# Another order for the end of a fused cross-attention kernel: turned maxima, normalised tiles, moments and gammas

## The chip, the cores and the metric

The kernel runs on one core of a Trainium2 chip. The metric is the device time of one execution in microseconds (us); the kernel's time is the median of several executions. A core has five engines that work side by side, each through its own instructions in order, and meet through semaphores: PE (TensorE, matrix products), DVE (VectorE), ACT (ScalarE), POOL (GpSimd) and SP (SyncE, here only for transfers). ACT issues a few transfers of its own.

## The reference

Cross-attention of 4 batches with 1024 queries, 64 keys and 16 heads of 16, then the output projection, the residual and a layer normalisation, all in float32:

```python
Q = _split_heads(jnp.einsum('bsd,ed->bse', query, w_q) + b_q)
K = _split_heads(jnp.einsum('bsd,ed->bse', key, w_k) + b_k)
V = _split_heads(jnp.einsum('bsd,ed->bse', value, w_v) + b_v)
scores = jnp.einsum('bhqd,bhkd->bhqk', Q, K) / jnp.sqrt(jnp.float32(D_K))
scores = jnp.where(mask[:, None, :, :] == 0, jnp.float32(-1000000000.0), scores)
attn = jax.nn.softmax(scores, axis=-1)
ctx = jnp.einsum('bhqk,bhkd->bhqd', attn, V)
ctx = ctx.transpose(0, 2, 1, 3).reshape(B, SQ, D_MODEL)
out = jnp.einsum('bsd,ed->bse', ctx, w_o) + b_o + residual
mu = jnp.mean(out, axis=-1, keepdims=True)
var = jnp.mean(jnp.square(out - mu), axis=-1, keepdims=True)
out = (out - mu) * jax.lax.rsqrt(var + LN_EPS) * ln_gamma + ln_beta
```

## The kernel before

The 4096 queries are cut into 8 chunks of 512 (CHUNKS; LAST is 7), each of 4 tiles of 128 queries. A chunk's 16 heads come in two groups, j = 0 and 1; "(c, j)" below is group j of chunk c. A chunk passes through these steps, several chunks being under way at once:

- PE projects the queries (project_queries, L361). ACT copies them out of PSUM (queries_out, queries_beside).
- max_scores(c, i), L406, gives the scores of one tile and group as queries by keys in a PSUM bank, eight per chunk (i = 0 to 7). DVE takes the maximum over the keys (maxima(c, i), L771). When all eight are there, PE turns the maxima (turn_max, L418, four transposes), and ACT copies them out negated (negative_max, L674, tile neg).
- PE makes the scores again as keys by queries: scores_on_mask (L445, L451), then scores_less_max (L458) adds the negated maxima. Where under(g) holds, the mask isn't added by PE (L445): ACT copies it into the four banks (mask_under, L668) as they come free behind the exponentials of the group before. ACT takes the exponentials in four quarters (exponentials(c, j), L658).
- PE multiplies with the values (values, L474). DVE turns the result (turn_out, L791), takes reciprocals, divides (L805) and turns the parts for the output product (L811): divide(c, j).
- PE applies wo (output(c, i, t), L500; i is a pair of tiles and t one of the pair). DVE adds the residual (residual(c, i), L819) and takes mean and variance (moments(c, i): two bn_stats L831, two bn_aggr L835).
- POOL makes rstd and shift out of these (deviations, L1003 to L1009), ACT applies them tile by tile (normalised(c, order), L681), POOL multiplies by gamma (L1023) and adds beta (L1026) for a pair of tiles (affine(c, i)), and SP stores.
- POOL also adds the output bias to x (with_bias, L994).

The steady loop runs over s from 0 to 5 on PE, DVE and POOL. Its pass s works on chunk s's scores, on the maxima of chunk s + 1, and on the outputs and normalisation of the chunks before. After it, the last steps are written out by hand, line by line, for each engine. The order on an engine is that of the code; an instruction waits for its semaphores and holds up everything behind it.

The last chunk is done otherwise at its end: the identity product of last_input (L513) brings x into PSUM, last_output adds the output product there, DVE takes the moments from PSUM, and centred (L841) and scaled (L851) do the normalisation on DVE. last_deviations on POOL gives the rstd. Of chunk 6, POOL does gammas and betas for tiles 0 and 1, and DVE (gammas, L858; betas, L864) for tiles 2 and 3, out of a PSUM copy of both rows that ACT makes once divide(7, 1) is over (L735). The stores of chunk 6 are issued by ACT (L739, L741), those of chunk 7 by SP (L266).

Waits that matter for the order: turn_max waits for all maxima of its chunk; output(5, 0) waits for all maxima of chunk 7; output(5, 1) for the neg of chunk 7; max_scores(7, 2) for maxima(7, 1); normalised(c, order) for the deviations of its tiles; last_input(0) and values(7, 1) for all exponentials; DVE's gammas for all normalised tiles of chunk 6.

Of the kernel before, what the change touches and what calls it, by code (L numbers as in the profile page):

```python
# [43 lines left out]
def build(nc, xT, x, maskT, ctxT, wq, wk, wv, wo, bias_rows, consts, out):  # L44
    with ExitStack() as ctx:
# [96 lines left out]
        stored = [sem(f"stored{i}") for i in range(2)]  # L142

        LAST = CHUNKS - 1
# [161 lines left out]
        def _(pe):  # L306
# [105 lines left out]
            def turn_max(c):  # L412
                pe.wait_ge(nm_done, HALVES * (c + 1))
                if c == 0:
                    pe.wait_ge(in_con, 16)
                    pe.wait_ge(kt_done, 2)
                for t in range(TILES):
                    mm = pe.transpose(ps_w[:, 1, t * P:(t + 1) * P], nmax[:, c % 2, t], con[:, IDENT:IDENT + P])  # L418
                mm.then_inc(turn_done, 1)
# [5 lines left out]
            def scores_on_mask(c, j):  # L425


                g = 2 * c + j
                b = c // PER_BATCH
                if g == 0:  # L430
                    pe.wait_ge(qe_done, 3)
                    pe.wait_ge(nm_done, HALVES)
                    pe.wait_ge(const_done, 2)
                    pe.wait_ge(kpair_done, 1)
                else:
                    if g == 1:
                        pe.wait_ge(kpair_done, 2)
                    pe.wait_ge(qe_done, g + 1)
                if not under(g):
                    if g:  # L440
                        pe.wait_ge(e_done, QUADS * g)
                    pe.wait_ge(mask_done, masks_done(c))
                    for quad in range(QUADS):
                        r = rows(quad % 2)
                        pe.matmul(ps_s[:, quad], key_rows[r].rearrange("p h k -> p (h k)"), mask[r, c % NM],  # L445
                                  start=True, stop=False)
                for quad in range(QUADS):
                    r = quad_rows(quad)
                    if under(g):
                        pe.wait_ge(under_done, QUADS * unders(g) + quad + 1)  # L450
                    pe.matmul(ps_s[:, quad], k_pair[r, b, j].rearrange("p h k -> p (h k)"), q_sb[r, c % NQ, j],  # L451
                              start=False, stop=False, skip_group_check=under(g))

            def scores_less_max(c, j):
                pe.wait_ge(neg_done, c + 1)
                for quad in range(QUADS):
                    r = slice(32 * quad, 32 * quad + 4)
                    pe.matmul(ps_s[:, quad], select[r, j].rearrange("p h k -> p (h k)"), neg[r, c % 2],  # L458
                              start=False, stop=True, skip_group_check=under(2 * c + j)).then_inc(s_done, 1)
# [126 lines left out]
            max_scores(LAST, 5)  # L586
            max_scores(LAST, 6)
            max_scores(LAST, 7)
            scores_on_mask(LAST, 0)
            output(LAST - 2, 0, 0)  # L590
            turn_max(LAST)
            output(LAST - 2, 0, 1)
            scores_less_max(LAST, 0)
            values(LAST - 1, 1)
            output(LAST - 2, 1, 0)
            output(LAST - 2, 1, 1)
# [12 lines left out]
        def _(act):  # L609
# [11 lines left out]
            def queries_out(c, j):  # L621
                act.wait_ge(q_done, 2 * c + j + 1)
                if c >= NQ:
                    act.wait_ge(s_done, PAIRS * (c - NQ + 1))
                    act.wait_ge(max_done, HALVES * (c - NQ + 1))
                act.activation(q_sb[:, c % NQ, j], query_bank(c, j), ACT.Identity,  # L626
                               bias=con[:, BIAS + j:BIAS + j + 1]).then_inc(qe_done, 1)
# [24 lines left out]
            def exponentials(c, j):  # L652
                g = 2 * c + j
                if g >= 2:
                    act.wait_ge(pv_done, PAIRS * (g - 1))
                for quad in range(QUADS):
                    act.wait_ge(s_done, QUADS * g + quad + 1)
                    act.activation(probs[:, g % 2, quad], ps_s[:, quad], ACT.Exp).then_inc(e_done, 1)  # L658
                    if quad and under(g + 1):
                        mask_under(g + 1, quad - 1)  # L660
                if under(g + 1):
                    mask_under(g + 1, QUADS - 1)
# [13 lines left out]
            def normalised(c, order=range(TILES)):  # L676
                act.wait_ge(ln_done, deviations_done(c, 2 in order))
                if c >= 2:
                    act.wait_ge(stored[c % 2], 16 * (c // 2))
                for t in order:  # L680
                    act.activation(y[:, c % 2, t], res[:, c % 2, t], ACT.Identity, bias=shift[:, c % 2, t:t + 1],  # L681
                                   scale=rstd[:, c % 2, t:t + 1]).then_inc(y_done, 1)
# [25 lines left out]
            for s in range(CHUNKS):  # L708
                exponentials(s, 0)
                if s < LAST:  # L710
                    queries_beside(s + 1, 1)
                if s == 0:
                    queries_out(2, 0)
                if s < 2:
                    high_x(s + 3)
                if 1 <= s and s + 2 < CHUNKS:
                    queries_out(s + 2, 0)
                exponentials(s, 1)
                if s + 2 < CHUNKS:
                    queries_beside(s + 2, 0)  # L720
                if s >= 2 and s + 3 < CHUNKS:
                    high_x(s + 3)
                if s == LAST:
                    normalised(LAST - 2, (0, 1))
                    normalised(LAST - 2, (2, 3))
                elif s == LAST - 1:
                    normalised(s - 2)
                if s + 2 < CHUNKS:
                    queries_out(s + 2, 1)
                if s + 1 < CHUNKS:  # L730
                    negative_max(s + 1)
                if 2 <= s < LAST - 1:
                    normalised(s - 2)
            act.wait_ge(div_done, GROUPS)
            act.activation(ps_s[:, 1].rearrange("p (n d) -> p n d", d=D), brow[:, 2:4], ACT.Copy).then_inc(gb_done, 1)  # L735
            normalised(LAST - 1, (0, 1))
            normalised(LAST - 1, (2, 3))
            act.wait_ge(dve_bet_done, 1)
            act.dma_start(out[LAST - 1, :, 2:4], y_of(LAST - 1)[:, 2:4]).then_inc(stored[(LAST - 1) % 2], 16)  # L739
            act.wait_ge(bet_done, 2 * LAST - 1)  # L740
            act.dma_start(out[LAST - 1, :, 0:2], y_of(LAST - 1)[:, 0:2]).then_inc(stored[(LAST - 1) % 2], 16)  # L741

        @block.vector
        def _(dve):
# [149 lines left out]
            for s in range(LAST - 1):  # L894
                front = s + 1
                maxima(front, 0)
                if s >= 2:
                    moments(s - 2, 0)
                maxima(front, 1)
                maxima(front, 2)  # L900
                if s >= 2:
                    residual(s - 2, 1)
                    turn_out(s - 1, 1)
                elif s == 0:
                    value_blocks()
                maxima(front, 3)
                if s >= 2:
                    divide_turned(s - 1, 1)
                elif s == 1:
                    divide(0, 1)  # L910
                maxima(front, 4)
                if s >= 2:
                    moments(s - 2, 1)
                maxima(front, 5)
                if s >= 1:
                    residual(s - 1, 0)
                maxima(front, 6)
                maxima(front, 7)
                divide(s, 0)
            maxima(LAST, 0)  # L920
            moments(LAST - 3, 0)
            maxima(LAST, 1)
            divide(LAST - 2, 1)
            residual(LAST - 3, 1)
# [27 lines left out]
        def _(pool):  # L952
# [65 lines left out]
                pool.tensor_tensor(rstd[:, i], veps[:, i], half_neg[:], ALU.pow).then_inc(ln_done, 1)  # L1018

            def affine(c, i):  # L1020
                two = slice(2 * i, 2 * i + 2)
                pool.wait_ge(y_done, TILES * c + 2 * i + 2)
                pool.tensor_tensor(y[:, c % 2, two], y[:, c % 2, two], brow[:, 2].unsqueeze(1).to_broadcast([P, 2, D]),  # L1023
                                   ALU.mult).then_inc(gam_done, 1)
                pool.wait_ge(gam_done, 2 * c + i + 1)
                pool.tensor_tensor(y[:, c % 2, two], y[:, c % 2, two], brow[:, 3].unsqueeze(1).to_broadcast([P, 2, D]),  # L1026
                                   ALU.add).then_inc(bet_done, 1)
# [43 lines left out]
            affine(LAST - 3, 0)  # L1071
            affine(LAST - 3, 1)
            deviations(LAST - 2, slice(0, 2))
            deviations(LAST - 2, slice(2, 4))
            affine(LAST - 2, 0)
            affine(LAST - 2, 1)
            deviations(LAST - 1, slice(0, 2))
            deviations(LAST - 1, slice(2, 4))
            last_deviations()
            affine(LAST - 1, 0)  # L1080


# [47 lines left out]
```

## Time and profile before

| | |
|---|---|
| time, median of 3 executions | 154.56 us (154.33 to 154.88) |
| the profiled execution | 154.85 us, of which the span of the profile is 153.3 us |
| busy, share of the span | PE 87%, DVE 81%, ACT 76%, POOL 68% |
| chain that ended last | PE 44%, DVE 27%, issue 8%, ACT 8%, DMA 5%, POOL 4% |
| granted PE clock | full until 146 us, half after it |

The span runs from the first instruction to the last event; about 1.5 us of the execution lie around it. Times of rows are from the start of the span. A busy share is an average over stages with different limits: the kernel's last fifth has to be read by itself. "Issue" in the chain is time in which the engine waited for nothing that the profile shows. The ends of matrix products are modelled, and spans on POOL are rough.

### The profile page before, as it was taken

The numbers are of one execution on the slowest core, as the hardware profiler recorded it, in microseconds if no ns is written. First come the engines' busy times: TensorE is split into PE (matmuls) and PEld (weight loads), VectorE is DVE, ScalarE is ACT, GpSimd is POOL, SyncE is SP. The second block draws the span as 40 slices with busy tenths as digits, with TensorE's granted clock in tenths as the row PEclk, the third lists the DMA queues.
The fourth block names the chain that finished last, engine by engine and source line by source line (L and its number), as shares of the span: only waits on it lengthen the run. The fifth ranks groups of instructions, "written<-read, shape, count | busy, mean of one in ns | idle before, by whom it ended". The sixth has DMA issues, their size and how long they took to land.

```text
span 153.3 us, 2741 instructions
## 1 busy us (share of the span) xinstructions
PE 133.6 (87%) x900; PEld 80.4 (52%) x900; DVE 123.8 (81%) x232; ACT 116.5 (76%) x210; POOL 103.9 (68%) x107
## 2 busy tenths in 40 slices
PE   0799997978899999999999999999988999999500
PEld 0586745453565656555665565546535355368400
DVE  0098938577878899898989898989899997999991
ACT  3269988898688878999999989999796786271320
POOL 6003738583499502399949999999849999479590
PEclk9999999999999999999999999999999999999955
DMA  4997299999953230029700570027300620300306
GB/s 139 322 283 208 50 275 236 266 290 266 218 209 73 80 122 19 0 85 266 265 6 0 139 261 14 2 56 220 137 0 4 175 98 0 141 0 0 137 17 259
DMA packets 8382, 20.46 MB, mean 133 GB/s; under 512 B 1073, under 2 KB 1329, under 8 KB 8369
## 3 DMA queue, kind: packets, MB, share of 16 engines
q1 hardware_dynamic: 7648, 19.14, 43.3%
q10 hardware_dynamic: 720, 1.15, 2.2%
q8 instruction: 7, 0.11, 0.3%
q14 instruction: 7, 0.05, 0.1%
HBM read 12.43 MB, written 4.19 MB: 108 GB/s over the span
## 4 chain that ended last, share of the span: by engine, by line
PE 44%; DVE 27%; issue 8%; ACT 8%; DMA 5%; POOL 4%; SPq 2%; DVEq 1%; POOLq 0%; ACTq 0%
PE ps_w L500 10%; PE ps_w L406 9%; DVE nmax L771 8%; PE ps_s L451 6%; PE ps_s L474 5%; DMA wv_sb<-wv 5%; DVE turned L791 5%; PE ps_w L361 5%; DVE stat L831 4%; DVE div_t L805 3%; PE ps_s L458 3%; DVE res L819 2%; ACT probs L658 2%; DVE cn L811 2%; PE ps_s L445 2%
## 5 line engine op out<-in xcount | busy, mean ns | idle before, releaser
L771 DVE TENSOR_REDUCE nmax<-ps_w 128x8 f32<-128x512 f32 x56 | 37.5, 677 | 14.0 <-PE ps_w L406 13.4
L658 ACT ACTIVATE probs<-ps_s 128x512 f32<-128x512 f32 x64 | 35.4, 597 | 11.6 <-PE ps_s L458 11.6
L958 POOL TENSOR_TENSOR xt_l<-xt_sb,xt_h 128x1024 fp32r<-128x1024 f32 x7 | 16.6, 2370 | 24.0 <-DVE k_half L759 10.9
L406 PEld LDWEIGHTS ps_w<-k_half,q_mask 128*128 128x128 f32 x112 | 16.8, 188 | 26.8 <-DVE nmax L771 20.8
L406 PE MATMUL ps_w<-k_half,q_mask 128*128 128x256 f32 x112 | 27.1, 331 | 4.1 <-DVE nmax L771 3.5
L500 PE MATMUL ps_w<-wo_sb,cn 128*128 128x256 f32 x112 | 29.0, 387 | 0.5
L668 ACT ACTIVATE ps_s<-mask 128x512 f32<-128x512 f32 x44 | 25.8, 612 | 0.0
L500 PEld LDWEIGHTS ps_w<-wo_sb,cn 128*128 128x128 f32 x112 | 19.4, 189 | 6.4 <-issue 2.7
L791 DVE STREAM_TRANSPOSE turned<-ps_s 128x1024 f32<-128x1024 f32 x16 | 19.9, 1242 | 0.1
L994 POOL TENSOR_TENSOR x_sb<-x_sb,brow 128x1024 f32<-128x1024 f32 x8 | 19.0, 2378 | 1.0 <-DMA x_sb<-x 0.8
L451 PE MATMUL ps_s<-q_sb,k_pair 32*128 32x512 f32 x128 | 19.3, 640 | 0.0
L1023 POOL TENSOR_TENSOR y<-y,brow 128x512 f32<-128x512 f32 x13 | 16.6, 1278 | 3.2 <-ACT y L681 3.0
L643 ACT ACTIVATE q_mask<-q_sb 64x512 fp32r<-64x512 f32 x28 | 17.6, 629 | 0.4
L474 PE MATMUL ps_s<-probs,v_bd 64*32 64x512 f32 x256 | 17.4, 601 | 0.0
L1026 POOL TENSOR_TENSOR y<-y,brow 128x512 f32<-128x512 f32 x13 | 16.6, 1276 | 1.0
L681 ACT ACTIVATE y<-res,shift,rstd 128x256 f32<-128x256 f32 x28 | 14.6, 596 | 2.3 <-POOL shift L1009 2.3
L811 DVE STREAM_TRANSPOSE cn<-div_t 128x512 f32<-128x512 f32 x16 | 11.4, 711 | 0.6
L626 ACT ACTIVATE q_sb<-ps_w,con 128x512 f32<-128x512 f32 x13 | 8.9, 682 | 3.3 <-PE ps_w L361 3.2
L805 DVE TENSOR_TENSOR div_t<-turned,ps_s 128x512 f32<-128x512 f32 x16 | 10.9, 683 | 0.4
L361 PE MATMUL ps_w<-xt_h,wq_h 128*128 128x512 f32 x26 | 10.6, 408 | 0.3 <-DVE nmax L771 0.3
L458 PE MATMUL ps_s<-neg,select 4*128 4x512 f32 x64 | 10.5, 643 | 0.4 <-ACT neg L674 0.3
L819 DVE TENSOR_TENSOR res<-ps_w,x_sb 128x512 f32<-128x512 f32 x14 | 9.5, 677 | 1.4 <-PE ps_w L500 0.9
(79 smaller groups left out, 198.2 us busy)
## 6 DMA issues: line engine op xcount, KB each, us to landing
x_sb<-x SPq DMA_DIRECT2D x8, 512.0 KB, 4.8
xt_sb<-xT SPq DMA_DIRECT2D x7, 512.0 KB, 5.1
q_mask<-mask SPq DMA_DIRECT2D x12, 256.0 KB, 4.1
out<-y SPq DMA_DIRECT2D x6, 512.0 KB, 2.6
m_sb<-maskT SPq DMA_DIRECT2D x16, 128.0 KB, 6.2
xt_sb<-xT SPq DMA_DIRECT2D x2, 256.0 KB, 5.6
q_mask<-mask SPq DMA_DIRECT2D x4, 128.0 KB, 2.3
out<-y ACTq DMA_DIRECT2D x2, 256.0 KB, 2.3
```

Of the source, the lines that this page charges most:

```text
L361: mm = pe.matmul(query_bank(c, j), w[:, d, j * P:(j + 1) * P], a[:, c % 2, d], start=d == 0 and w is wq_h and a is xt_h, stop=d == PC - 1 ...
L406: mm = pe.matmul(max_bank(c, i)[:, half * 256:half * 256 + 256], q_mask[:, c % 2, half, j, t * P:(t + 1) * P], k_half[:, b % 2, half, j].r ...
L451: pe.matmul(ps_s[:, quad], k_pair[r, b, j].rearrange("p h k -> p (h k)"), q_sb[r, c % NQ, j], start=False, stop=False, skip_group_check=un ...
L474: pe.matmul(values_banks(g)[quad_rows(quad), h], v_bd[rows(h), b, QUADS * j + quad], probs[rows(h), g % 2, quad], start=True, stop=True).t ...
L500: return pe.matmul(tile_outputs(c, i)[:, t], cn[:, c % 2, j, (2 * i + t) * P:(2 * i + t + 1) * P], wo_sb[:, j], start=j == 0 and c < LAST, ...
L643: act.activation(q_mask[r, c % 2, half, j], q_sb[r, c % NQ, j], ACT.Copy).then_inc(qdir_done, 1)
L658: act.activation(probs[:, g % 2, quad], ps_s[:, quad], ACT.Exp).then_inc(e_done, 1)
L668: act.activation(ps_s[:, quad], mask[:, g // 2 % NM].bitcast(F32), ACT.Copy).then_inc(under_done, 1)
L771: dve.tensor_reduce(nmax[:, c % 2, t].rearrange("p (q r) -> p q r", r=32)[:, :, 2 * j:2 * j + 2], max_bank(c, i).rearrange("p (q h k) -> p ...
L791: dve.transpose(turned[:, 0:2 * CHUNK], values_banks(g).rearrange("p h n -> p (h n)")).then_inc(pturn_done, 1)
L958: pool.tensor_tensor(xt_l[:, c % 2], xt_sb[:, c % 2], xt_h[:, c % 2].bitcast(F32), ALU.subtract).then_inc(xl_done, 1)
L994: pool.tensor_tensor(x_sb[:, c % 3], x_sb[:, c % 3], brow[:, 1].unsqueeze(1).to_broadcast([P, TILES, D]), ALU.add).then_inc(xb_done, 1)
```

## The change

In the steady loop DVE takes moments(4, 0) in pass s = 5, between maxima(6, 6) and maxima(6, 7), and not after maxima(7, 0). On PE, turn_max(7) follows max_scores(7, 7) at once, and both parts of scores(7, 0) come after output(5, 0). On ACT, normalised(4) comes behind the neg copy of chunk 7 and not ahead of it; the first two tiles of chunk 5 are normalised ahead of exponentials(7, 1), the other two behind it as before; the stores of the two halves of chunk 6 change places. On POOL, affine is split into gammas and betas, and in chunks 5 and 6 the gammas of the first pair run between the two sets of deviations, the betas behind the second set (in chunk 6 behind last_deviations).

```diff
 PE:
             max_scores(LAST, 7)
-            scores_on_mask(LAST, 0)
+            turn_max(LAST)
             output(LAST - 2, 0, 0)
-            turn_max(LAST)
             output(LAST - 2, 0, 1)
-            scores_less_max(LAST, 0)
+            scores(LAST, 0)
             values(LAST - 1, 1)
 ACT:
+                if s == LAST:
+                    normalised(LAST - 2, (0, 1))
                 exponentials(s, 1)
...
                 if s == LAST:
-                    normalised(LAST - 2, (0, 1))
                     normalised(LAST - 2, (2, 3))
-                elif s == LAST - 1:
-                    normalised(s - 2)
...
                     negative_max(s + 1)
-                if 2 <= s < LAST - 1:
+                if 2 <= s < LAST:
                     normalised(s - 2)
...
+            act.wait_ge(bet_done, 2 * LAST - 1)
+            act.dma_start(out[LAST - 1, :, 0:2], y_of(LAST - 1)[:, 0:2]).then_inc(stored[(LAST - 1) % 2], 16)
             act.wait_ge(dve_bet_done, 1)
             act.dma_start(out[LAST - 1, :, 2:4], y_of(LAST - 1)[:, 2:4]).then_inc(stored[(LAST - 1) % 2], 16)
-            act.wait_ge(bet_done, 2 * LAST - 1)
-            act.dma_start(out[LAST - 1, :, 0:2], y_of(LAST - 1)[:, 0:2]).then_inc(stored[(LAST - 1) % 2], 16)
 DVE:
                 maxima(front, 6)
+                if s == LAST - 2:
+                    moments(s - 1, 0)
                 maxima(front, 7)
                 divide(s, 0)
             maxima(LAST, 0)
-            moments(LAST - 3, 0)
             maxima(LAST, 1)
 POOL:
             def affine(c, i):
+                gammas(c, i)
+                betas(c, i)
...
             deviations(LAST - 2, slice(0, 2))
+            gammas(LAST - 2, 0)
             deviations(LAST - 2, slice(2, 4))
-            affine(LAST - 2, 0)
+            betas(LAST - 2, 0)
             affine(LAST - 2, 1)
             deviations(LAST - 1, slice(0, 2))
+            gammas(LAST - 1, 0)
             deviations(LAST - 1, slice(2, 4))
             last_deviations()
-            affine(LAST - 1, 0)
+            betas(LAST - 1, 0)
```

## Rows read from the trace of the kernel before

**Rows 1.** The page: the chain of work that ended last, shares by engine.
```profile
PE 44%; DVE 27%; issue 8%; ACT 8%; DMA 5%; POOL 4%; SPq 2%; DVEq 1%; POOLq 0%; ACTq 0%
```
**Rows 2.** Busy time by stretch: us, engines' busy time, clock, DMA share, GB/s.
```profile
128.15:141.30 13.15, 13.15 (x101) 8.00 (x92) 12.52 (x26) 6.07 (x12) 10.01 (x14) 1.00 0.11 41
```
**Rows 3.** Timeline, DVE: start, duration, line, operation, tiles, [idle before].
```profile
109.72 0.69 DVE L771 TENSOR_REDUCE nmax<-ps_w 128x8 f32<-128x512 f32 x1 [0.65 <-PE ps_w L406]
...
113.93 0.73 DVE L831 BATCH_NORM_STATS2 stat<-res 128x6 f32<-128x256 f32 x2
...
114.86 0.66 DVE L771 TENSOR_REDUCE nmax<-ps_w 128x8 f32<-128x512 f32 x1
...
120.57 3.34 DVE L771 TENSOR_REDUCE nmax<-ps_w 128x8 f32<-128x512 f32 x5
```
**Rows 4.** Timeline, PE, around the turn of chunk 6's maxima.
```profile
110.89 0.60 PE L418 MATMUL ps_w<-con,nmax 128*128 128x128 f32 x4
...
115.58 0.51 PE L406 MATMUL ps_w<-k_half,q_mask 128*128 128x256 f32 x2 [1.07 <-DVE nmax L771]
```
**Rows 5.** Timeline, PE and DVE, after the last maxima.
```profile
126.17 0.60 PE L418 MATMUL ps_w<-con,nmax 128*128 128x128 f32 x4
...
127.67 0.69 DVE L819 TENSOR_TENSOR res<-ps_w,x_sb 128x512 f32<-128x512 f32 x1 [0.74 <-PE ps_w L500]
...
128.00 1.09 PE L474 MATMUL ps_s<-probs,v_bd 64*32 64x512 f32 x16
...
129.02 1.99 PE L500 MATMUL ps_w<-wo_sb,cn 128*128 128x256 f32 x8
```
**Rows 6.** Timeline, PE, ACT and DVE, last scores to last divide.
```profile
131.61 1.14 PE L451 MATMUL ps_s<-q_sb,k_pair 32*128 32x512 f32 x8
...
132.91 1.09 PE L474 MATMUL ps_s<-probs,v_bd 64*32 64x512 f32 x16
133.06 2.07 ACT L658 ACTIVATE probs<-ps_s 128x512 f32<-128x512 f32 x4 [2.85 <-PE ps_s L458]
...
134.29 1.25 DVE L791 STREAM_TRANSPOSE turned<-ps_s 128x1024 f32<-128x1024 f32 x1
...
135.76 1.03 PE L513 MATMUL ps_s<-x_sb,con 128*128 128x256 f32 x4
...
138.96 1.22 DVE L791 STREAM_TRANSPOSE turned<-ps_s 128x1024 f32<-128x1024 f32 x1
```
**Rows 7.** Timeline, POOL: chunk 4's gammas and betas, chunk 5's first deviations.
```profile
125.48 1.28 POOL L1023 TENSOR_TENSOR y<-y,brow 128x512 f32<-128x512 f32 x1
...
128.06 1.29 POOL L1023 TENSOR_TENSOR y<-y,brow 128x512 f32<-128x512 f32 x1
...
129.43 1.27 POOL L1026 TENSOR_TENSOR y<-y,brow 128x512 f32<-128x512 f32 x1
...
130.78 0.19 POOL L1003 TENSOR_SCALAR veps<-mv 128x2 f32<-128x2 f32 x1
...
132.11 0.19 POOL L1009 TENSOR_TENSOR shift<-nmean,rstd 128x2 f32<-128x2 f32 x1
```
**Rows 8.** Timeline, POOL, ACT and DVE: the last deviations, tiles and gammas.
```profile
141.46 0.19 POOL L1003 TENSOR_SCALAR veps<-mv 128x2 f32<-128x2 f32 x1
...
143.78 0.19 POOL L1003 TENSOR_SCALAR veps<-mv 128x2 f32<-128x2 f32 x1 [0.79 <-DVE mv L835]
...
145.32 1.09 ACT L681 ACTIVATE y<-res,shift,rstd 128x256 f32<-128x256 f32 x2 [1.21 <-POOL shift L1009]
...
145.91 1.01 POOL L1018 TENSOR_TENSOR rstd<-veps,half_neg 128x4 f32<-128x4 f32 x1
...
147.01 0.68 DVE L858 TENSOR_TENSOR y<-y,ps_s 128x512 f32<-128x512 f32 x1
```
**Rows 9.** Timeline, ACT's first store; then busy time by stretch, the stores' end.
```profile
148.44 0.36 ACTq L739 DMA_DIRECT2D out<-y  x1
...
152.00:152.30 0.30, 0.00 (x0) 0.00 (x0) 0.00 (x0) 0.00 (x0) 0.00 (x0) 0.50 0.47 171
```

More of the change, by code:

```diff
@@ L1020, in affine, with gammas @@
             def affine(c, i):
+                gammas(c, i)
+                betas(c, i)
+            def gammas(c, i):
                 two = slice(2 * i, 2 * i + 2)
@@ L1024, in affine, with betas @@
                                    ALU.mult).then_inc(gam_done, 1)
+            def betas(c, i):
+                two = slice(2 * i, 2 * i + 2)
                 pool.wait_ge(gam_done, 2 * c + i + 1)
```

## The prediction

> **What bounds the kernel now.** I read the page first, for the order of size: three engines are busy for three quarters of the span or more, and the chain of work that ended last is mostly PE and DVE, with POOL at 4% [rows 1]. An average of that kind can't price a change to the last fifth of the kernel, so I went on to the busy time by stretch, then to the timeline of each engine from 94 us on, and last to the waits. In the stretch from 128.15 to 141.30 DVE works 12.52 of 13.15 us and PE all 13.15, ACT and POOL much less [rows 2]. What to see in the timeline is which engine has no gap: after the wait of 0.74 us at 127.67 [rows 5] DVE runs nearly without one to the last scaled tiles, and the end is DVE's: chunk 6's gammas at 147.01, then betas, then the two scaled pairs, then the stores [rows 8, 9]. POOL stands idle in several places in that end. It therefore costs nothing today, and what I have to find out is whether it still costs nothing in the new order.
>
> **Chunk 4's moments a step sooner.** The pair of moments takes a slot of 0.93 us (113.93 to 114.86) [rows 3]. In its new place, before maxima(6, 7), DVE sat idle for 0.65 us waiting for PE [rows 3]. So 0.65 of it is hidden and maxima(6, 7) moves back by 0.28, to end at 110.69. The turn_max behind it starts at 110.89 because PE is busy with projections until then [rows 4], so 0.2 us of cover is left and it isn't late. If that cover were gone, the delay would be that of neg and the scores of chunk 6, behind which PE has a wait anyway. Later, maxima(7, 1) comes 0.93 - 0.28 = 0.65 earlier. PE waited 1.07 us for just that at 115.58 [rows 4], so the whole row behind it (output of chunk 4, scores of chunk 6, exponentials, maxima(7, 2) to (7, 7)) moves with it: the last maximum ends at 120.57 + 3.34 - 0.65 = 123.26 instead of 123.91 [rows 3]. Bounds: 0, if the later steps are held elsewhere, and 0.93. I take 0.65, because the idle time is on the row itself. SP's load of the last x waits for a residual of this row and comes earlier too; nobody is late for it.
>
> **Last maxima turned at once.** turn_max goes ahead of the scores on mask and of output(5, 0, 0). It starts at 123.30 instead of 126.17 and takes 0.60 [rows 5]. The neg copy starts on ACT at 123.94. ACT now has normalised(4) behind it and not ahead. ACT instructions follow each other at 0.49 us (four exponentials in 2.07 [rows 6]), so chunk 4 is normalised from 124.43, its first two tiles at 1.09 [rows 8] are there at 125.52, and POOL, with a hand-over of 0.08, begins affine(4, 0) at 125.60. Before it was 125.48 [rows 7]. **This is the first cost: 0.12 us on POOL**, although everything ahead came 0.65 earlier, since normalised(4) lost its place ahead of neg.
> On PE, output(5, 0) runs from 123.9 for 1.99 us at most (a pair of tiles in [rows 5]) to 125.8, and the 0.74 us that DVE stood still for residual(5, 0) vanish. Then the scores of (7, 0): exponentials follow the start of scores by 1.45 and values by 1.30 (131.61 to 133.06 and 132.91 [rows 6]), so values(6, 1) begins at 127.0 to 127.2 instead of 128.00 [rows 5]: 0.8 to 1.0 earlier. DVE took values(7, 0) 1.38 after they began (134.29 against 132.91 [rows 6]); with the whole PE row 0.8 to 1.0 earlier, it now takes them at 133.3 to 133.5, and would be ready for divide(7, 1) at 138.0 to 138.2 instead of 138.96 [rows 6].
>
> **Chunk 5's tiles ahead of the last scores' exponentials.** ACT is idle 2.85 us before exponentials(7, 1) [rows 6], and the two activations go there. But they wait for the deviations of (5, 0), which POOL begins only behind affine(4): 125.60 + (130.78 - 125.48 = 5.30) = 130.90, and the shift ends 1.52 later (130.78 to 132.11 plus 0.19 [rows 7]) at 132.42. The two tiles then run from 132.46 and exponentials(7, 1), which could have begun at 132.1 to 132.3, are queued behind them until 133.44: 0.38 later than the 133.06 of before. They end at 135.51. The identity products of last_input(0) (1.03 [rows 6]) and 1.38 for the values give DVE its data at about 137.9, when DVE itself is ready at 138.0 to 138.2. So the queueing is just covered; that cover is 0.1 to 0.3 us. DVE's own end is then about 0.8 early. But last_input(0) starts at 135.55 instead of 135.76 [rows 6], so PE's row to the last output products is 0.2 early only, and DVE's last moments have to wait for them; between 0.2 and 0.8 I estimate 0.5, which lets DVE's gammas start at 146.5.
>
> **GpSimd's gammas between deviations.** From 132.42 I follow POOL. Prices: gamma to its beta 1.37 (128.06 to 129.43), beta to the next gamma 1.21 (2.58 from gamma to gamma, 125.48 to 128.06, less 1.37), to the next deviations 1.35 (129.43 to 130.78), a set of deviations 1.52 [rows 7]. Tiles (5, 0) normalised at 133.55, gammas(5, 0) from 133.63; deviations(5, second) 134.98 to 136.50; betas(5, 0) 136.5; gammas(5, 1) 137.72, betas(5, 1) 139.09; deviations(6, first) 140.44 to 141.96. Before, POOL lost time here in waits for DVE and ACT, and this set began at 141.46 [rows 8]: 1.0 is gained. ACT normalises from 142.00 to 143.09. And now the new order takes it back: gammas(6, 0) stand ahead of the second deviations, wait for ACT and run from 143.17; **deviations(6, second) begins at 144.52 where it began at 143.78** as soon as DVE's means were there [rows 8]. They end at 146.04, ACT normalises the last two tiles at 146.08 to 147.17 (before from 145.32), and DVE's gammas, which wait for these, start at 147.22 instead of 147.01 [rows 8]. Behind that wait DVE's betas and all of the last chunk's scaling are queued: **+0.21 us**. The limit at the end has changed from DVE to the round POOL, ACT, POOL, ACT, DVE.
> For a gamma followed by deviations there is no row; I took beta to deviations, 1.35. The nearest ends are 1.21 and 1.37, for two places -0.28 to +0.04. The Trainium skill (GPSIMD Engine Reference, on completion under the instruction's steps) says that completion holds back what waits on the instruction's semaphore and not the next Pool instruction; by that the veps behind a gamma, which doesn't depend on it, would start at the short distance and the sum would be -0.07 instead of +0.21. The row of beta to deviations, where nothing depends either, shows 1.35, so I keep the row's number.
>
> **The stores.** ACT now issues the store of tiles 0 and 1 of chunk 6 first, and it waits for betas(6, 0), which POOL runs last: 146.04, then 0.27 to rstd, 1.01 for it [rows 8] and 1.27 for the betas = 148.6, and the other half queues behind that. The first store before went at 148.44 [rows 9]. The four stores then run back to back until 152.3 [rows 9], so a first issue 0.2 later moves the end by as much, the same as DVE's part; the two are side by side, not added.
> By the Trainium skill (DMA: Bandwidth & Descriptors, on the fixed cost) each transfer has about 2.0 us fixed and 436 GB/s, so 0.25 MB issued last ends 2.6 us after its issue however early the others went. By that, an early DVE alone would bring the end forward even if POOL's store is late.
>
> **Sum.** On the profiled execution of 154.85 us: + 0.21 = 155.06. That execution stands 0.29 us above the median of 154.56, so 154.77, rounded 154.8 us, 0.1% more.
>
> **Rivals.** (1) *Faster: POOL doesn't hold the end.* DVE goes on at 146.5, gain 0.5: 154.05. It needs the round above to be 0.72 us shorter than my sum; the short distances of POOL give 0.28 and the best case of the moved moments 0.28 (0.93 instead of 0.65), together 0.56, so only with both and something more. At 0.56 alone the time is 154.2. Against it are POOL's durations, which hardly vary. (2) *Slower: the step of moments gives nothing.* Place: the wait of 1.07 at 115.58. If PE or ACT holds the row behind it, the last maximum stays at 123.91, neg, normalised(4) and POOL's whole series shift one for one, and the end is 0.21 + 0.65 = 0.86 later: 155.4. It decides (over 155.02) from a saving below 0.40 instead of 0.65. The cover of 0.2 at 110.89 and PE's gap of 1.07 speak against it. (3) *It cancels:* 154.55, with POOL's distances short, gains and losses nearly zero. (4) *The exponentials become the bound:* exponentials(7, 1) later than about 134.5 instead of 133.44 would make DVE the last again; POOL would then be late itself, so it is a part of (2).
>
> **Numbers.** My forecast (154.65 to 155.02) 0.40; (3) and down to 154.10, 0.17; (1) below 154.10, 0.17; (2) above 155.02, 0.26. A measurement here can tell 0.3%, 0.46 us, from nothing: faster is below 154.10, slower above 155.02. The range for 8 in 10 is 154.05 to 155.45, from rival (1) to rival (2).
>
> **What would show it.** Right: turn_max directly after the last maximum, near 123.3; no gap on DVE before residual(5, 0); exponentials(7, 1) near 133.4 behind two activations of L681's kind that waited for POOL's shift; POOL without a gap from 125.6 to 132.4; deviations(6, second) near 144.5; a DVE gap of about 0.8 near 146.5, ended by ACT's y; first store at 148.6. Wrong: no such gap and gammas before 146.8 (then rival 1), or maxima(7, 7) still ending at 123.9 (rival 2).

## The result, and the profile after

The changed kernel took 155.19 us in the median of 22 executions (154.19 to 156.25), the kernel before beside it 154.52 (154.24 to 156.11): ratio 1.0043, 95% interval 1.0022 to 1.0063. By that number the change costs 0.66 us. The forecast was 154.8, +0.21, within 154.05 to 155.45. So the range holds, the sign is right, and the size is three times the forecast. The trace shows that these 0.66 us have two sources.

The page of the changed kernel's profiled execution (156.25 us, span 154.7), the slices of granted PE clock and the chain that ended last by engine:

```profile
PEclk9999997899999999999999999999999999999965
...
PE 38%; DVE 24%; POOL 11%; issue 9%; ACT 8%; DMA 5%; SPq 2%; DVEq 1%; POOLq 0%; ACTq 0%
```

Two things are new. POOL's share of the chain is 11% where it was 4% [rows 1]: that is the change. And there is a 7 in the clock line near a sixth of the span, far ahead of all changed code. Busy time by stretch shows it, first this trace, where the clock is 1.00 at full rate (2.4 GHz) and 0.5 at half (1.2 GHz):

```profile
21.00:25.00 4.00, 3.05 (x21) 1.51 (x20) 1.69 (x3) 3.41 (x8) 3.51 (x3) 1.00 0.97 283
25.00:29.00 4.00, 4.00 (x16) 2.79 (x20) 2.26 (x4) 2.45 (x4) 1.22 (x3) 0.57 1.06 260
```

The granted clock is at half from 25.1 to 28.5 us here; PE was busy 3.05 of the 4.00 us before. The projection products take 0.63 us each in that stretch instead of 0.40. What it costs is read from the first of them to the scores behind them, this trace first, then that of before:

```profile
24.85 0.58 PE L361 MATMUL ps_w<-xt_h,wq_h 128*128 128x512 f32 x1 [0.29 <-DVE nmax L769]
...
30.13 0.73 PE L406 MATMUL ps_w<-k_half,q_mask 128*128 128x256 f32 x4
```
```profile
25.06 0.47 PE L361 MATMUL ps_w<-xt_h,wq_h 128*128 128x512 f32 x1 [0.29 <-DVE nmax L771]
...
28.80 0.74 PE L406 MATMUL ps_w<-k_half,q_mask 128*128 128x256 f32 x4
```

That is 5.28 against 3.74 us, so the half clock costs 1.54 us. As this trace was 0.21 ahead before it, 1.33 is left behind it. Up to the changed code both kernels run the same instructions, and still chunk 6's sixth maximum stands at 108.32 in this trace and at 107.01 in that of before: **1.31 us are lost before the change begins**. Read with that shift, the end is close to the forecast:

```profile
124.54 0.66 PE L418 MATMUL ps_w<-con,nmax 128*128 128x128 f32 x4 [0.79 <-DVE nmax L769]
...
127.43 0.65 DVE L817 TENSOR_TENSOR res<-ps_w,x_sb 128x512 f32<-128x512 f32 x1
...
133.75 1.09 ACT L680 ACTIVATE y<-res,shift,rstd 128x256 f32<-128x256 f32 x2 [3.38 <-POOL shift L1008]
134.75 2.03 ACT L657 ACTIVATE probs<-ps_s 128x512 f32<-128x512 f32 x4
...
145.78 0.19 POOL L1002 TENSOR_SCALAR veps<-mv 128x2 f32<-128x2 f32 x1
...
148.45 0.69 DVE L856 TENSOR_TENSOR y<-y,ps_s 128x512 f32<-128x512 f32 x1 [0.42 <-ACT y L680]
```

DVE's gap before residual(5, 0) is gone (0.74 at 127.67 [rows 5]); ACT waits 3.38 us for POOL's shift where it waited 2.85 for the scores [rows 6]; the second deviations of chunk 6 begin 2.00 later than in [rows 8], of which 1.31 is the shift; and DVE's gammas have a gap in front of them, ended by ACT's y, where there was none: 148.45 against 147.01 [rows 8], +1.44, of which 0.13 is left for the change.

The executions say the same. Nine of the 22 of the changed kernel have a mean granted clock of 0.967 to 0.969, the profiled one among them, and take 155.62 us or more; of the kernel before, whose clocks aren't listed here, one of 22 is as slow (156.11). Without these ten the medians are 154.68 (13 executions) and 154.48 (21): +0.20.

### The profile page after: what moved, and what is told of

Same layout as the page of the kernel before. It is cut to its first block, busy times and chain, and to the rows that moved or that the text cites. A ratio compares the mean times of both kernels' runs of the same rounds, so it can differ in the third digit from the quotient of the medians.

```text
span 154.7 us, 2741 instructions
## 1 busy us (share of the span) xinstructions
PE 134.1 (87%) x900; PEld 80.4 (52%) x900; DVE 124.1 (80%) x232; ACT 116.6 (75%) x210; POOL 103.8 (67%) x107
## 4 chain that ended last, share of the span: by engine, by line
PE 38%; DVE 24%; POOL 11%; issue 9%; ACT 8%; DMA 5%; SPq 2%; DVEq 1%; POOLq 0%; ACTq 0%
PE ps_w L406 9%; DVE nmax L769 8%; PE ps_w L500 6%; PE ps_w L361 6%; DMA wv_sb<-wv 5%; PE ps_s L474 5%; DVE turned L789 5%; PE ps_s L451 4%; POOL y L1026 4%; POOL y L1032 3%; DVE div_t L803 3%; DVE stat L829 2%; ACT y L680 2%; DVE res L817 2%; PE ps_s L458 2%
## 5 line engine op out<-in xcount | busy, mean ns | idle before, releaser
L451 PE MATMUL ps_s<-q_sb,k_pair 32*128 32x512 f32 x128 | 18.2, 640 | 0.0
L361 PE MATMUL ps_w<-xt_h,wq_l 128*128 128x512 f32 x26 | 10.7, 411 | 0.0
```

Source lines behind the costliest of these rows:

```text
L361: mm = pe.matmul(query_bank(c, j), w[:, d, j * P:(j + 1) * P], a[:, c % 2, d], start=d == 0 and w is wq_h and a is xt_h, stop=d == PC - 1 ...
```

## Experiments

**1. How much is the change, how much the clock.** Both kernels once more, unchanged, in one series with all else:

> The kernel before once more, as a control that lists the granted clock of each of its executions. Theory 1 (the new end costs 0.13 us and the rest of the measured +0.66 us comes from a stretch of half clock near 25 us that some executions have and others have not): executions fall in groups by mean clock, about 154.4 us at 0.977 or more without that stretch and about 155.8 at 0.967 with it, in this kernel too; ratio to the kernel before 1.000. Rival (the change itself costs 0.66): all executions within 154.2 to 155.0 and none at 0.967.

> The changed kernel once more. Theory 1: the executions at a mean clock of 0.977 or more take 154.4 to 154.8 us, within 0.2 us of those of the kernel before at the same clock; those at 0.967 take 155.6 to 156.3. Rival (the change costs 0.66 by itself): the executions at 0.977 take 155.1 or more.

The kernel before took 154.53 us (12 executions), the changed one 154.68 (12). Sorted by the mean granted clock of each execution:

| mean clock | kernel before, this series | beside it, 35 executions | changed kernel, this series | changed kernel, first measurement |
|---|---|---|---|---|
| 0.985 to 0.988 | 5, median 154.07 | 8, 154.38 | 5, 154.28 | 3, 154.36 |
| 0.975 to 0.978 | 4, 154.58 | 12, 154.62 | 6, 154.92 | 7, 154.68 |
| 0.979 to 0.982 | 2, 154.82 | 8, 155.03 | none | 3, 155.32 |
| 0.967 to 0.969 | 1, 155.52 | 7, 155.92 | 1, 155.78 | 9, 155.82 |

The stretch of half clock isn't a property of the change: the kernel before has such executions, 7 of 35 (and 8 of 35 beside the second series). In the first measurement 9 of 22 executions of the changed kernel were at 0.967 to 0.969, and of the kernel before only one was as slow as these (156.11). The unequal share is where most of the +0.66 comes from; the rival, by which the kernel before has no such executions and the changed one takes 155.1 or more at 0.977, is out. Within this series the medians of the changed kernel at equal mean clock lie between 0.14 below and 0.34 above those of the kernel before, so theory 1 holds within what such small groups can tell. The two whole medians don't differ either: to the 35 executions beside them (154.86) the ratios are 0.9984 (0.9956 to 1.0012) for the kernel before and 0.9978 (0.9948 to 1.0007) for the changed one.

The mean clock is a rough label. It falls with an early stretch, but also when the clock goes to half earlier at the end, where PE has nothing left to do: at 146 us in the first trace of before (0.977), at 148 in that of this series (0.985). And the traces differ ahead of that: the first one of before lies 0.80 later (107.01 against 106.21 at chunk 6's sixth maximum), and is as late at 20 us already, at full clock. No run here shows what makes such an execution late at its start. Small differences below are therefore read from traces that agree up to the change.

The two profiled executions of this series have the same mean clock, 0.985, and no early stretch, and their sixth maxima of chunk 6 stand at 106.21 and 106.22, so they can be laid side by side. Timeline of DVE, chunk 6's last maximum, the last five maxima and chunk 6's gammas, the kernel before:

```profile
108.91 0.69 DVE L771 TENSOR_REDUCE nmax<-ps_w 128x8 f32<-128x512 f32 x1 [0.64 <-PE ps_w L406]
...
119.76 3.34 DVE L771 TENSOR_REDUCE nmax<-ps_w 128x8 f32<-128x512 f32 x5
...
146.20 0.68 DVE L858 TENSOR_TENSOR y<-y,ps_s 128x512 f32<-128x512 f32 x1
```

The changed kernel, DVE and POOL:

```profile
109.16 0.66 DVE L769 TENSOR_REDUCE nmax<-ps_w 128x8 f32<-128x512 f32 x1
...
119.15 3.24 DVE L769 TENSOR_REDUCE nmax<-ps_w 128x8 f32<-128x512 f32 x5
...
142.38 1.26 POOL L1026 TENSOR_TENSOR y<-y,brow 128x512 f32<-128x512 f32 x1 [1.21 <-ACT y L680]
...
142.46 0.76 DVE L829 BATCH_NORM_STATS2 stat<-ps_s 128x6 f32<-128x256 f32 x2 [0.42 <-issue]
...
143.73 0.19 POOL L1002 TENSOR_SCALAR veps<-mv 128x2 f32<-128x2 f32 x1
...
146.41 0.69 DVE L856 TENSOR_TENSOR y<-y,ps_s 128x512 f32<-128x512 f32 x1 [0.44 <-ACT y L680]
```

The moved moments delay one maximum by 0.25 and bring the last five 0.6 forward; POOL's gammas of chunk 6 (142.38) stand ahead of its second deviations (143.73, in the control 142.97); at the end DVE's gammas start at 146.41 instead of 146.20: **+0.21 us, the forecast's own term**. The spans are 152.7 us (changed) and 152.5 (control).

**2. The moments alone.**

```diff
 kernel before, DVE
                 maxima(front, 6)
+                if s == LAST - 2:
+                    moments(s - 1, 0)
                 maxima(front, 7)
...
             maxima(LAST, 0)
-            moments(LAST - 3, 0)
             maxima(LAST, 1)
```

> The kernel before with one part of the change: chunk 4's moments between maxima(6, 6) and (6, 7). If this step gives the 0.65 us of the prediction and nothing at the end takes it back: last maximum at 123.26 where it was 123.91, chunk 6's gammas on DVE at 146.4 instead of 147.0, time 0.65 us less, 153.9. If the step gives nothing (prediction's rival 2): no change, last maximum at 123.9 on the scale of the trace before. Executions compared at the same mean clock.

153.92 us (12), ratio 0.9939 (0.9911 to 0.9968) to the kernel before. DVE's gammas:

```profile
145.47 0.68 DVE L858 TENSOR_TENSOR y<-y,ps_s 128x512 f32<-128x512 f32 x1
```

They start 0.73 before the 146.20 of the control (the trace is aligned with it up to 108 us), a little more than the 0.65 expected, and nothing at the end takes it back. The prediction's rival 2 is out.

**3. GpSimd's gammas and the stores.** The changed kernel with chunk 6's gammas behind both deviations again, once with the old order of the stores (first run) and once with the changed one (second run):

```diff
 changed kernel, POOL
             deviations(LAST - 1, slice(0, 2))
-            gammas(LAST - 1, 0)
             deviations(LAST - 1, slice(2, 4))
             last_deviations()
-            betas(LAST - 1, 0)
+            affine(LAST - 1, 0)
 ACT (first run only)
-            act.wait_ge(bet_done, 2 * LAST - 1)
-            act.dma_start(out[LAST - 1, :, 0:2], ...)
             act.wait_ge(dve_bet_done, 1)
             act.dma_start(out[LAST - 1, :, 2:4], ...)
+            act.wait_ge(bet_done, 2 * LAST - 1)
+            act.dma_start(out[LAST - 1, :, 0:2], ...)
```

> The changed kernel with gammas(6, 0) back behind both sets of deviations (affine(6, 0) at the end, as before) and the two stores of chunk 6 in their old order. If POOL's gammas ahead of the second deviations set the end (prediction): these deviations begin about 142.8 instead of 144.5 on the scale of the trace before, DVE's gammas near 146.5 without a gap before them, first store 148.0, time 0.5 to 0.7 us under the changed kernel at the same mean clock. If the end is set elsewhere: no change.

> The changed kernel with gammas(6, 0) moved back, but the stores in the changed order (POOL's half first, the DVE half queued behind it on ACT). DVE's gammas at 145.9 as in the run that also has the old store order. If the end is the four stores back to back from their start, the transfers start near 149.0 instead of 148.2 and the end and the time are 0.6 to 0.8 us later than in that run. If the end hangs on the last issue alone (fixed time after it), both are the same within 0.2 us.

With the old store order: 154.59 us (12), ratio 0.9980 (0.9943 to 1.0016) to the kernel before, of which 5 executions at 0.968 to 0.970; at 0.987 and 0.988 four executions with a median of 153.84, against 154.28 of the changed kernel at 0.985 to 0.987: 0.44 less, a little under the expected 0.5 to 0.7. POOL and DVE:

```profile
142.19 0.19 POOL L1002 TENSOR_SCALAR veps<-mv 128x2 f32<-128x2 f32 x1 [0.94 <-DVE mv L833]
...
145.94 0.68 DVE L856 TENSOR_TENSOR y<-y,ps_s 128x512 f32<-128x512 f32 x1
```

The second deviations now start as soon as DVE has the means (142.19 instead of 143.73) and DVE's gammas have no gap: 0.47 earlier. With the changed store order instead: 154.98 us (10), ratio 1.0017 (0.9989 to 1.0046), none below 0.975. This trace lies 0.93 later from early on, and so do its gammas, again without a gap:

```profile
146.87 0.68 DVE L856 TENSOR_TENSOR y<-y,ps_s 128x512 f32<-128x512 f32 x1
```

This run differs from the changed kernel by the gammas alone, so that POOL held DVE's gammas is shown. What differs between the two runs is the way from there to the end of the span: 152.2 - 145.94 = 6.26 us in the run with the old store order, 153.8 - 146.87 = 6.93 here. The first issue of ACT, and the busy time of the DMA engines at the end (last columns: DMA share, GB/s), changed order:

```profile
149.38 0.35 ACTq L737 DMA_DIRECT2D out<-y  x1
...
149.50:150.00 0.50, 0.00 (x0) 0.00 (x0) 0.33 (x1) 0.00 (x0) 0.00 (x0) 0.50 0.17 61
150.00:150.50 0.50, 0.00 (x0) 0.00 (x0) 0.00 (x0) 0.00 (x0) 0.00 (x0) 0.50 1.03 385
...
152.50:153.00 0.50, 0.00 (x0) 0.00 (x0) 0.00 (x0) 0.00 (x0) 0.00 (x0) 0.50 0.36 123
```

Here the four stores of 256 KB run without a pause at 365 to 393 GB/s (with the old order nearly so, one half microsecond at 316), so the end is set by when the first of them starts. The store of POOL's half, put first, has to wait for the betas that POOL now ends at 149.35 (148.09 + 1.26), and it holds DVE's half, ready since 148.3 (146.87 + 0.71 + 0.69), until 149.77 behind it. The first transfer under way is then one of chunk 7's, issued by SP at 149.07, where in the other run it was DVE's half, issued at 147.38: 1.69 later, of which 0.93 is the shift. The last issue is SP's second in both, over at 149.27 and at 150.19, so it is later by no more than the shift and can't be what moved the end. The change's own order of the stores is harmless only as long as gammas(6, 0) run early: the two parts belong together.

**4. Chunk 5's tiles and the early turn.** Both start from the run with the old stores. First POOL's whole old order (affine(5, 0) behind the second deviations as well), then also chunk 5's tiles behind the last exponentials:

```diff
 POOL (both runs)
             deviations(LAST - 2, slice(0, 2))
-            gammas(LAST - 2, 0)
             deviations(LAST - 2, slice(2, 4))
-            betas(LAST - 2, 0)
+            affine(LAST - 2, 0)
 ACT (second run)
-                if s == LAST:
-                    normalised(LAST - 2, (0, 1))
                 exponentials(s, 1)
...
                 if s == LAST:
+                    normalised(LAST - 2, (0, 1))
                     normalised(LAST - 2, (2, 3))
```

> The changed kernel with all of POOL's order and the two stores as before (affine(5, 0) and affine(6, 0) whole again); the first two tiles of chunk 5 still ahead of exponentials(7, 1). POOL then has slack, so whether gammas(5, 0) stand between the deviations is free: exponentials(7, 1), PE's wait of 0.87 before last_input(0), DVE's gap of 0.42 before the last moments and its gammas at 145.9 all as in the run with only gammas(6, 0) moved back; time within 0.15 us of that run at the same clock. If the split in chunk 5 gave something, this is slower than that run.

> As the run with POOL's old order, and chunk 5's tiles all behind exponentials(7, 1) again: of the change only the moved moments, the early turn_max with output(5, 0) ahead of the scores, and normalised(4) behind neg are left. If the tiles ahead of the exponentials cost PE and DVE their lead (a part of the prediction), exponentials(7, 1) begin at 131.1 instead of 132.7, PE has no wait before last_input(0), DVE no gap before the last moments and its gammas begin at 145.1, 0.8 us earlier; against the run with the moments alone (gammas at 145.5) 0.4 us earlier, which is the worth of the early turn. Time about 0.4 us under the moments alone at the same clock. If the early turn gives nothing, it equals the moments alone.

These two and the run with the changed store order are of a second series, in which the kernel before took 154.55 us (35 executions) where it took 154.86 in the first; medians of the two series are compared with that in mind.

The first: 154.06 us (10), ratio 0.9980 (0.9956 to 1.0004); five executions at 0.986 to 0.988 have a median of 153.87, against 153.84 of the run before. Its trace lies 0.28 later than that run's before the change begins and 0.26 at the last maxima, and its gammas 0.27 later:

```profile
146.21 0.68 DVE L856 TENSOR_TENSOR y<-y,ps_s 128x512 f32<-128x512 f32 x1
```

So the end is the same: the split of chunk 5's gammas is worth nothing.

The second: 153.65 us (12), ratio 0.9951 (0.9924 to 0.9978). PE, ACT and DVE:

```profile
131.10 2.07 ACT L657 ACTIVATE probs<-ps_s 128x512 f32<-128x512 f32 x4 [2.84 <-PE ps_s L458]
...
133.79 1.03 PE L513 MATMUL ps_s<-x_sb,con 128*128 128x256 f32 x4
...
141.64 0.73 DVE L828 BATCH_NORM_STATS2 stat<-ps_s 128x6 f32<-128x256 f32 x2
...
145.04 0.68 DVE L855 TENSOR_TENSOR y<-y,ps_s 128x512 f32<-128x512 f32 x1
```

The first two places in the changed kernel (the third, DVE's last moments, is 142.46 in its rows above):

```profile
132.68 2.04 ACT L657 ACTIVATE probs<-ps_s 128x512 f32<-128x512 f32 x4
...
134.86 1.10 PE L513 MATMUL ps_s<-x_sb,con 128*128 128x256 f32 x4 [0.88 <-ACT probs L657]
```

Without the tiles ahead, exponentials(7, 1) begin at 131.10 and not at 132.68, PE has no wait of 0.88 before the identity products, DVE no gap of 0.42 before its last moments, and the gammas begin at 145.04: 0.90 before those of the run with only chunk 6's gammas moved back, 0.8 when the 0.10 is taken off by which that trace was later before the change. Against the moments alone (145.47) they are 0.43 earlier, which is the early turn with output(5, 0) ahead of the scores and normalised(4) behind neg. This version is 1.16 us before the control at the gammas and 1.2 us in the span (151.3 against 152.5); it is ahead of the kernel before in the ratio too. In the median it is only 0.27 under the moments alone, and in the ratio not ahead of them (0.9951 against 0.9939, intervals overlapping; 3 of 12 executions at 0.971 and 0.972 against 2 of 12): that it beats the moments alone rests on one trace of each.

**5. The half clock.** Three small products in PE's idle times ahead of it, written to a part of a bank that nothing reads:

```diff
 changed kernel, PE, pass s = 0
+            def filler(n):
+                for _ in range(n):
+                    pe.matmul(ps_s[rows(1), 4, 0:D], ctx_t[:, 0, 0], wv_sb[:, 0], start=True, stop=True)
...
                 max_scores(front, 1)
+                if s == 0:
+                    filler(2)
...
                 elif s == 0:
+                    filler(1)
                     project_queries(ahead, 0)
```

> The changed kernel with three small products of PE added in its idle times near 23.5 and 24.6 us, into a part of a bank that nothing reads (the output is not touched by them). If the half clock from 25.1 to 28.5 us, which some executions show, hangs on PE's idle times ahead of it, no execution has it any more: all at a mean clock of 0.976 or more, none above 155.3 us, median 154.4 to 154.8. If it has another cause, a part of the executions (1 to 5 of 12) stays at 0.967 to 0.971 and above 155.4 us.

None of 12 executions was below 0.976, where the changed kernel alone had 10 in 34 (9 of 22 and 1 of 12). If that were the rate, chance would give none in 12 with a probability of 0.71 to the power of 12, under 2%. But the runs of the same series, whose code is the same up to there, had fewer at 0.972 or less: 8 of 35, 0 of 10, 1 of 10 and 3 of 12, together 12 of 67, and at that rate none in 12 comes by chance in 9 of 100 cases. One of them had none in 10 without any added product. The expected time was missed, though: the median is 155.42, and at 0.976 to 0.978 it is 155.6 against 154.7 to 154.9 without the products. They took 1.08 and 0.65 us on PE, more than the idle times that they were to fill:

```profile
23.92 1.08 PE L527 MATMUL ps_s<-wv_sb,ctx_t 128*64 128x256 f32 x4
24.93 0.50 PE L406 MATMUL ps_w<-k_half,q_mask 128*128 128x256 f32 x2
25.36 0.65 PE L527 MATMUL ps_s<-wv_sb,ctx_t 128*64 128x256 f32 x2
```

So the result fits an effect of PE's idle time there, and doesn't show it: the added products also move everything behind them, and no run told these apart. And by its median this filler costs 0.7 us more than the changed kernel of the series before took (155.42 against 154.68).

## Why the prediction was right, and where it was off

Positions are those of the aligned traces; the scale of the prediction is 0.81 later (its 147.01 is 146.20 here).

- **Moments a step sooner: 0.65 forecast, 0.6 at the last five maxima and 0.73 at DVE's gammas measured.** The wait that hides it and the wait of PE behind it were read rightly; PE's 1.07 us at 115.58 [rows 4] fell to 0.35, and turn_max of chunk 6 didn't move (110.10 in both).
- **The first cost on POOL** (affine(4, 0) 0.12 later, since normalised(4) lost its place ahead of neg): measured -0.13 (124.80 against 124.93 in the control), with POOL idle 0.46 before it, waiting for ACT's y as forecast. The place itself was right (124.79 on this scale). The control's own load of x was late and had held POOL for 0.59; in the first trace that wait was 0.37. So the sign of this term hangs on a transfer.
- **Tiles ahead of the exponentials.** Forecast: queued until 133.44, 0.38 later than before, just covered on DVE. Measured: 132.68 against 132.25, 0.43 later. The cover of 0.1 to 0.3 wasn't there: DVE has a gap of 0.16 before divide(7, 1). DVE's lead at divide(7, 1) is 0.89 (137.27 against 138.16), for 0.8 to 1.0 forecast. The 0.5 us that I left of it by DVE's gammas, an estimate between 0.2 and 0.8, measured 0.26 (145.94 in the run where POOL doesn't hold them, against 146.20). This term was mis-sized by half: I gave PE's last output products a lead of 0.2, and they have none (139.61 against 139.62), and DVE stands still for 0.42 before its last moments. The profile names no releaser for this gap; the code waits there for these products, and where they began at 138.46 (fourth experiment) there is no gap. It made DVE's gap before its gammas smaller, 0.44 for a forecast of about 0.8, and didn't matter for the total, as POOL came later still. That was luck: had POOL been shorter, the forecast of rival 1 (gain 0.5) would have been too high by half.
- **Gammas between deviations.** Forecast 144.52, on this scale 143.71; measured 143.73. DVE's gammas forecast +0.21, measured +0.21. The distance from gamma to deviations was bounded at 1.21 to 1.37 and taken at 1.35; it is 1.35 (142.38 to 143.73). The rule of the Trainium skill (GPSIMD Engine Reference, Instruction dispatch) on completion, as I applied it, would have put it at the short distance: the trace disagrees with that reading.
- **The stores.** First issue at 147.88 against 147.63, +0.25 for a forecast of +0.2. By the fixed cost of the Trainium skill (DMA: Bandwidth & Descriptors, Anatomy of one DMA), which that page gives for transfers issued by GpSimd, only the last issue would count; the run with the stores' changed order decides for the four in a row, with 0.67 us.
- **The total.** In the two traces that agree up to the change +0.21 at DVE's gammas; in the group at 0.985 to 0.988 of one series +0.21 (154.28 against 154.07), in that at 0.975 to 0.978 +0.34, and in the whole medians +0.15 (154.68 against 154.53), with intervals that don't tell them apart. The measured +0.66 is this and a larger share of executions with a stretch of half clock in the fill of the pipeline. No step of the sum held a term for that, and the trace of before showed nothing of it: one profiled execution can't show what happens in one of five. What I named as noise, 0.3%, is too small for a kernel whose executions fall in groups 1.3 us apart. That 155.19 still lies inside the range, which was drawn for other rivals, is in part luck.

By its parts, each read at DVE's gammas on top of the ones before it, the change is: moments -0.73, early turn -0.43, chunk 5's tiles ahead of the exponentials +0.90, split of chunk 5's gammas 0, chunk 6's gammas between the deviations (with the stores in the order that suits them) +0.47. The sum, +0.21, comes out by construction, and the traces agree before the change only to 0.1 us: +0.8 and +0.55 is as good a reading of the last two that cost. Two good steps were paid for by two that put a waiting instruction ahead of work that was ready.

Still open is why the first measurement had the half clock in 9 of 22 executions of the changed kernel and in one of 22 of the other. Both kernels run the same code until then, and the next series had it in 1 of 12 of each and in 7 of 35 beside them. Over all runs the share goes from 0 of 10 to 9 of 22; that the change makes the stretch likelier is neither shown nor ruled out.

## What to carry to other kernels

An engine with idle time costs nothing only in the order it has now: before moving a waiting instruction ahead on an in-order engine, follow what is queued behind it on that engine, and price the round over the other engines until it comes back. When a change of several parts moves the time by little, take it apart in aligned traces: here parts of about -1.2 and +1.4 us were hidden in +0.21. And before a difference of half a per cent is put down to the code, look at the granted clock of each execution, and at whether the traces agree up to the changed code: equal mean clock alone doesn't make two executions alike.

## What the runs showed of the hardware that I had not expected

Executions of one and the same kernel differ by whether the PE clock is granted at half for 3.4 us near 25 us (25.07 to 28.48 in the trace shown), where PE had been busy 3.05 of 4 us; it cost 1.5 us in that trace, and the groups of executions with and without it lie 1.3 us apart (155.92 against 154.62). In traces with the full clock PE had been busy 3.06 of the same 4 us, so that number alone doesn't tell when it falls. And four stores of 256 KB issued within 1.1 us from two queues (149.07 to 150.19) moved at 365 to 393 GB/s as one stream, so that the later first store made a later end, by 0.67 us.
